# Node pass of a graph network: map pairs in one scatter, roots on ScalarE, stores issued by SyncE

## The reference, cut to what matters

```
# a layer for a node without edges (the part that the node pass computes for every node)
x1 = norm(relu(norm(x @ W1b + b1)) @ W2 + b2 + x)              # layer 0
x2 = norm(gelu(norm(x1 @ W + bias)) + x1)                      # layer 1
h  = elu(elu(elu(x2 @ Wl1 + b) @ Wl2 + b) @ Wlin + blin)       # layer 2
x3 = norm(h + x2)
x4 = norm(x3)                                                  # layer 3 adds nothing
def norm(y): return (y - mean(y)) / sqrt(var(y) + 1e-5)
```

## Time and profile before

| | us |
|---|---|
| runs | 4839.3, 4844.04, 4848.83; median 4844.04 |
| profiled execution: device time | 4839.3 |
| profiled execution: span | 4837.6 |
| node pass (from its first instructions to the first of slot pass 0) | 64.91 to 1669.33 |
| busy over the span: PE, DVE, ACT, POOL | 3813.0, 3637.8, 3183.7, 3089.0 |

### The profile page before, as it was taken

How to read it: one execution, slowest core, us unless ns; L and a number is a source line. 1 busy time by engine, 2 the same in 40 slices (tenths; PEclk the granted TensorE clock), 3 DMA queues, 4 the chain that set the end, 5 groups by cost and what they waited for, 6 DMA issues and landing times. The chain is left out here.

```text
span 4837.6 us, 74788 instructions
## 1 busy us (share of the span) xinstructions
PE 3813.0 (79%) x19896; PEld 2560.8 (53%) x20115; DVE 3637.8 (75%) x5894; ACT 3183.7 (66%) x10636; POOL 3089.0 (64%) x3645
## 2 busy tenths in 40 slices
PE   3888888888888699999688886888867777576676
PEld 3666666666666456666465564555534444344444
DVE  3666566666666488888599996999979999577776
ACT  2888888888887578888588885555545555333333
POOL 4889898898998577777444442333234443477775
PEclk9999999999999799999799998999989999788888
DMA  2334334334433333333233332333334433333221
GB/s 68 103 106 109 106 104 112 105 109 111 111 107 95 99 85 94 91 89 82 69 87 88 90 89 63 106 106 107 96 77 107 107 107 89 84 83 83 82 80 48
DMA packets 695838, 451.77 MB, mean 93 GB/s; under 512 B 143539, under 2 KB 623257, under 8 KB 695696
## 3 DMA queue, kind: packets, MB, share of 16 engines
q1 hardware_dynamic: 219504, 182.41, 14.0%
q10 hardware_dynamic: 413392, 186.30, 13.5%
q0 software_dynamic: 62800, 81.68, 7.0%
HBM read 253.00 MB, written 199.90 MB: 94 GB/s over the span
## 5 line engine op out<-in xcount | busy, mean ns | idle before, releaser
L769 POOL TENSOR_TENSOR node_rstd<-node_variance,minus_half 128x4 f32<-128x4 f32 x588 | 650.1, 1109 | 13.5 <-DMA slot_map<-node_value,node_index 1.4
L224 ACT ACTIVATE node_z<-psum 128x128 f32<-128x128 f32 x1960 | 513.5, 277 | 156.7 <-PE psum L204 87.6
L230 DVE TENSOR_TENSOR node_x<-psum,node_rstd 128x512 f32<-128x512 f32 x294 | 202.9, 690 | 487.2 <-POOL node_rstd L769 487.2
L1153 POOL DMA_INDIRECT slot_src_rows<-x,slot_index x392 | 450.8, 1150 | 168.5 <-issue 104.5
L919 POOL DMA_INDIRECT slot_map<-node_value,node_index x392 | 417.6, 1065 | 74.5 <-issue 73.5
L224 ACT ACTIVATION_READ_ACCUMULATOR node_z<-psum 128x1 f32 x1960 | 407.0, 208 | 0.0
L224 ACT ACTIVATE slot_logit<-psum 128x128 f32<-128x128 f32 x980 | 256.7, 280 | 198.0 <-PE psum L204 197.9
L1153 POOL DMA_INDIRECT slot2b_src_rows<-xl,slot2b_index x196 | 249.1, 1271 | 81.8 <-issue 46.2
L213 PE MATMUL psum<-ident,node_x 128*128 128x128 f32 x784 | 140.0, 306 | 193.9 <-DVE node_x L230 193.4
L1139 POOL DMA_INDIRECT out_nodes<-slot_new,slot_side_index x196 | 228.0, 1163 | 91.6 <-POOL slot_side_index L1133 43.8
L204 PE MATMUL psum<-center,slot_t 128*128 128x128 f32 x1176 | 215.1, 285 | 81.5 <-DVE slot_t L1592 52.7
(11 more groups left out here) (400 smaller groups left out, 12778.7 us busy)
## 6 DMA issues: line engine op xcount, KB each, us to landing
x<-node_x ACTq DMA_DIRECT2D x294, 256.0 KB, 2.7
slot_keep<-keep SPq DMA_DIRECT2D x147, 256.0 KB, 3.9
node_xT<-in_x_T SPq DMA_DIRECT2D x98, 256.0 KB, 3.4
out_nodes<-node_x ACTq DMA_DIRECT2D x98, 256.0 KB, 3.0
x<-slot_new ACTq DMA_DIRECT2D x98, 256.0 KB, 2.4
slot_dst_rows<-x SPq DMA_DIRECT2D x98, 256.0 KB, 4.3
staged<-node_gathered ACTq DMA_DIRECT2D x14, 896.0 KB, 5.9
xl<-node_xl ACTq DMA_DIRECT2D x98, 128.0 KB, 3.8
```

The lines of the kernel that those rows point to most:

```text
L224: ins = act.activation(g.z[u][:, t, :], rows[:, t, :], ACT.Square, scale=float(D ** -0.5), accum_out=g.mean_square[u][:, t:t + 1])
L230: v.tensor_tensor(out[:, :, :], source, g.rstd[u][:, :].unsqueeze(2).broadcast_to([P, TILES, D]), ALU.mult)\
L769: pool.tensor_tensor(g.rstd[u][:, :], g.variance[u][:, :], g.c.minus_half[:, :], ALU.pow).then_inc(g.pool_out[u], 1)
L1153: pool.indirect_dma_start(src_rows[u][:, t, 0:src_width], None, table, at_index(index[u][:, t:t + 1], 0))\
```

## The change

Six edits, all for the node pass:

- The two scatters per tile become one of a pair of numbers (8 bytes per node). Both orders use the index list of the last slot; the mirrored number of that target's first slot is now computed in `prepare` on DVE, and some tables there are no longer made.
- The norms `sq0`, `sq2` and `sq4` take their root on ACT (`_log`, then `_rstd` as exp). `sq1` and `sq3` stay on POOL.
- The squares of `x3` are dropped. With r the factor of the fifth norm, the variance of `x3` is 1 - eps x r^2, so DVE computes r^2 and then 1 + eps - eps x r^2 on 128x4 tiles, and POOL its power -0.5.
- All stores go to SP, in the plan's order, together with the loads. The gathered rows are stored per unit (two tiles), no longer once per iteration.
- Gathers and scatters are steps of the chain: `gather0`, `gather1`, `put0`, `put1` of every unit stand together in POOL's order.
- The order is a new plan with period 12.80. Table loads are put by the program, as in the slot passes. Wherever a table load is not needed for a step, none is put.

```
-        "node": (6.61, (2.400, 2.660, 3.600, ...), (0.01, 0.55, 1.50, 3.45, 3.86, 6.01)),
+        "node": (12.80, (4.154, 2.724, 12.612, ..., 98.077, 91.997, 97.903, 7.365, 7.370, 7.375, 7.380, 0.000), ()),

+def norm_on_act(tag, out):
+    return [("ACT", tag), ("ACT", tag + "_log"), ("ACT", tag + "_rstd"), ("DVE", out)]
+def norm_on_pool(tag, out):
     return [("ACT", tag), ("POOL", tag + "_eps"), ("POOL", tag + "_rstd"), ("DVE", out)]

+NODE_CHAIN = [("SP", "load"), ("PE", "h0")] + norm_on_act("sq0", "z0") + [("PE", "z0T"), ("ACT", "relu0"), ("PE", "y0")] + \
+    norm_on_pool("sq1", "x1") + [("SP", "store_x1"), ...] + norm_on_act("sq2", "z1") + \
...
+    norm_on_act("sq4", "x3") + [("SP", "store_x3"), ("DVE", "square"), ("DVE", "var5"), ("POOL", "rstd5"), ("DVE", "x4"),
+                                ("SP", "store_x4"), ("POOL", "gather0"), ("POOL", "gather1"), ("POOL", "put0"), ("POOL", "put1"),
+                                ("SP", "store_staged")]

# SP
+                if step == "load":
+                        sp.wait_ge(*g.PE.done(u, i - 1, "y0"))
+                    sp.dma_start(xT[u][:, :], ...).then_inc(x_loaded[u], 16)
+                elif step == "store_x1":
+                    sp.wait_ge(*g.DVE.done(u, i, "x1"))
+                    sp.dma_start(rows_in_table(dram.x1, i, u), x1[u][:, :, :]).then_inc(x1_stored[u], 16)
...
+                elif step == "store_staged":
+                    sp.wait_ge(gathers_done[u], (i + 1) * 16 * SIDE)
+                    sp.dma_start(dram.staged[...], gathered[u][:, :, :]).then_inc(staged[u], 16)

# ACT
+                elif what == "log":
+                    act.wait_ge(*g.ACT.done(u, i, tag))
+                    act_copy(act, g, u, g.variance[u][:, :], g.mean_square[u][:, :], ACT.Ln, c.eps[:, 0:1])
+                elif what == "rstd":
+                    act.wait_ge(*g.ACT.done(u, i, tag + "_log"))
+                    act_copy(act, g, u, g.rstd[u][:, :], g.variance[u][:, :], ACT.Exp, scale=-0.5)

# DVE
+                elif step == "square":
+                    v.tensor_tensor(g.raw[u][:, :], g.rstd[u][:, :], g.rstd[u][:, :], ALU.mult)
+                elif step == "var5":
+                    v.tensor_scalar(var5[u][:, :], g.raw[u][:, :], -LN_EPS, 1.0 + LN_EPS, ALU.mult, ALU.add)

# POOL
-                    pool.indirect_dma_start(dram.slot_map_flat, at_index(index[k][:, t:t + 1], 0),
-                                            value[k - 1][:, t:t + 1], None, bounds_check=2 * N - 1, ...)
+                    pool.indirect_dma_start(dram.slot_map, at_index(dst_index[:, t:t + 1], 0), value[:, t, :], None,
+                                            bounds_check=N - 1, oob_is_err=False).then_inc(scattered, 16)
+                elif step == "rstd5":
+                    pool.tensor_tensor(rstd5[u][:, :], var5[u][:, :], c.minus_half[:, :], ALU.pow)

# prepare, VectorE, at its end
+            v.tensor_scalar(c.payload[:, :, 1], first_col[:, :], -1.0, float(N_PAD + E_PAD - 1), ALU.mult, ALU.add)
```

More of the change, by code:

```diff
@@ L173, in plan @@
         steps.names = [step for of, step in chain if of == engine and not step.startswith(UNCOUNTED)]
-UNCOUNTED = ("store", "index", "gather", "dst_index", "dst_gather", "keep_map", "scatter")
+UNCOUNTED = ("store", "index", "gather", "put", "dst_index", "dst_gather", "keep_map", "scatter")
 def tiles_of(t):
@@ L627, in pe_node @@
[L627 to L674, removed]
@@ L677, in act_node @@
[L677 to L712, removed]
-    if step == "store_x3":
-        act.wait_ge(*g.DVE.done(u, i, "x3"))
-        act.dma_start(g.rows_in_table(c.dram.x3, i, u), g.x3[u][:, :, :]).then_inc(g.x3_stored[u], 16)
@@ new lines, in act_table, with table_for @@
+def act_table(act, nc, loaded, wanted):
+    if loaded not in wanted:
+        act.add_instruction(mybir.InstLoadActFuncSet(name=nc.get_next_instruction_name(), ins=[], outs=[],
+                                                     act_func_set_id=wanted[0]))
+        return wanted[0]
+    return loaded
+def table_for(step):
+    if step in ("e0", "e1"):
+        return (EXP_SET,)
+    if step.endswith("_log"):
+        return (LOG_SET,)
+    if step == "gelu1":
+        return (GELU_SET,)
+    if step.startswith("exp") or step.endswith("_rstd"):
+        return (LOG_SET, EXP_SET)
+    return None
@@ L779, in node_pass @@
         phase_tiles(ctx, nc, g, "node", NODE_STREAMS, primed=1)
-        g.A = g.B = lambda u: c.psum[:, u, :]
-        gathers = [(0, t) for t in range(SIDE_TILES)]
-        scatters = [(k, t) for t in range(SIDE_TILES) for k in (1, 2)]
-        plan(g, NODE_CHAIN, "node", gathers + scatters)
-        middle = [n for n, item in enumerate(g.order) if item[3] == scatters[4]][0]
-        g.order = [(-1, 0, "POOL", "side_index")] + g.order[:middle] + [(-1, 0, "ACT", "stage")] + g.order[middle:] + \
-            [(-1, 0, "POOL", "side_end")]
@@ L838, in run @@
+            settled = table_at_end(g)
             def run(i, part):
+                loaded = settled if part == "all" else None
                 for u, i, step in turns(g, "ACT", i, part):
-                    if step == "stage":
-                        stage(i)
-                    else:
-                        act_node(act, g, u, i, step)
-                    if step == "sq5":
-                        act.wait_ge(*g.DVE.done(u, i, "x3"))
-                        act_squares(act, g, u, g.x3[u])
@@ L862, in run @@
             def run(i, part):
                 for u, i, step in turns(g, "PE", i, part):
-                    pe_node(pe, g, u, i, step)
-            run(0, "in")
-            with pe.Fori(1, NODE_ITERS) as i:
-                run(i, "all")
-            run(NODE_ITERS, "out")
+                    work(u, i, step)
+            whole(pe, run)
         @block.vector
@@ L1280, in work @@
                         .then_inc(stored[u], 16)
-            wants = [table_for(step) for _, _, of, step in g.order if of == "ACT" and table_for(step)]
-            settled = None
-            for wanted in wants + wants:
-                settled = settled if settled in wanted else wanted[0]
+            settled = table_at_end(g)
             def run(i, part):
```

430 lines of the change are left out of this document (246 added, 184 removed), and 12 rows, old and new, of tables (NODE_CHAIN, PLAN).

## The result

| | before | after |
|---|---|---|
| median of four runs | 4843.0 us | 4551.2 us |
| profiled execution, device time | 4839.3 | 4551.07 |
| profiled execution, span | 4837.6 | 4549.4 |
| node pass in the profiled execution | 1604.4 | 1319.8 |

The ratio is 0.9399, with a 95% interval of 0.9384 to 0.9414. The changed kernel is 292 us faster; the forecast was 4593, with a range from 4543 to 4690.

What follows compares the result with a forecast made beforehand. POOL bounds the node pass now, ACT afterwards at 12.84 us per unit; 97 x 13.1 + 85 = 1356, 248 less than 1604, gives 4591 for an execution like the profiled one, 4593 as a middle, range 4543 to 4690.

Steps and rivals of the forecast that it cites:

- POOL as the bound before: Node pass of the old kernel: POOL's queue sets the pace, its groups filling 15.61 of 15.94 us per unit.
- POOL after the change: POOL's remaining powers, adds, gathers and scatters in the node pass: 8.9 us per unit, 7 less.
- the dearer scatter: Pair scatter on POOL priced at the two it replaces, 2.53 us: 11.4 us per unit, still not bounding.
- ScalarE as the next bound: ACT in the changed node pass: its work sums to a floor of 12.84 us per unit.
- Rival (c): ACT's table switches cost more than they show: ACT stays at 15.6 per unit, no change, 4833 us; chance 0.02.
- the store issues at 0.38 each: Five store issues on ACT before, 1.9 us per unit, counted in its 14.35; they leave with the change.
- PE: PE in the changed node pass: floor 11.9 us per unit at clock 1.00, 12.6 at 0.94; 1.00 expected.
- rival (a): PE or mutual waits bound the node pass: period 13.97 us, 164 us gained, 4675 us; chance 0.24.
- SP's queue: Loop through SP's in-order stores and loads: 23.3 us per two units, 11.6 each, hidden under 12.84.
- Rival (b): SP's wait ahead of the load makes the node pass slower: 17.9 us per unit, +217, 5056 us; chance 0.03.
- Period: Node pass time per unit after the change: 13.1 us, ACT's floor plus 2%.
- Ends: Fill, drain and barrier of the node pass: 85 us after the change, between 58 and 110; 58.2 before.

## Why the prediction was right, point by point

**POOL as the bound before.** Right. Taking 2.5 us per unit from POOL alone shortened the period by 2.3, and moving the stores alone shortened nothing.

**POOL after the change.** Right in size: its groups come to 9.5 us per unit with their gaps (8.9 forecast), and the pair scatter to 1.31, close to the lower bound that was taken. Wrong in one inference, that the dearer scatter at 11.4 per unit "still does not bound": with two scatters the time rose by 38 us, though POOL's sum was below ScalarE's.

**ScalarE as the next bound.** Right: 12.84 forecast, 12.71 measured, no wait for another engine, and +1.13 for 1.17 of added work. That the sum came so close was partly luck. Read from the same stretch (805.70 to 818.41), the five groups of squares take 5.37 where 5.00 was forecast; ln and exp take 1.30 (1.56), the copy of `xl` 0.26 (0.43), the two wide functions 1.46 (1.56), the three exps 1.72 (1.71) and the two table switches 2.60 (2.58). An error of +0.37 stood against errors of -0.53.

The Trainium skill, "ScalarE: Activation LUTs", section on what ACT_TABLE_LOAD costs, adds about 1.38 to each table switch. The trace again shows 1.30 for load and start of the next function together, so the estimate by the page, 2 x 1.38 = 2.8 us per unit more, would have been too high by that much. Rival (c) did not come.

**The step that failed: the store issues at 0.38 each.** "ACT had ... 14.35 before" was too high. The kernel before with one scatter has the same work on ScalarE: 12.7 us per unit busy, and 13.4 with all that is put down to "issue". In the changed kernel the five issues returned to ScalarE cost 0.28 per unit, not 1.9. The forecast's own show why: the issue of 0.38 starts at 814.88 and the table load beside it at 814.94. The claim that without the stores' move and the dropped squares "the gain would be small" is refuted too: the kernel before with one scatter has neither, and it has 230 of the 291 us. The error did not reach the forecast of the time, since the floor after the change contains no stores.

**PE.** Right that it does not bound and that the clock rises: it was 1.00 with PE busy 95%. The floor of 11.9 was 0.4 too low: PE is busy 953.0 / 77.2 = 12.3 us per unit, and 12.3 again at a period of 12.48, where it is full. So rival (a) did not come, but the margin under ScalarE's 12.7 was 0.4 and not 0.9.

**SP's queue.** No sign of the loop was seen: landings of `xT` have a median of 3.5 us and PE does not wait for them. The 2.3 us for queueing behind stores was not seen in that median. Rival (b) did not come.

**Period.** 13.1 forecast, 12.95 measured. The 2% put on the floor for waits stands for something else: no wait for another engine, but 0.24 us per unit of a gap once per iteration, which went when the loop was written out. Size: 97 x 0.15 = 15 us.

**Ends: the term that was most off.** 85 forecast, 1319.8 - 97 x 12.95 = 64 measured, within the bounds but far from the value taken. By the forecast's own test (the stage off by over 25 us; it is off by 36, of which 15 come from the period) this step was wrong. The timeline of SP shows where, in the loads of `xT` and the stores of `x4` of the first unit, of a unit in the steady part and of the last one:

```profile
70.52 0.45 SPq L706 DMA_DIRECT2D node_xT<-in_x_T  x1
144.77 0.37 SPq L721 DMA_DIRECT2D out_nodes<-node_x  x1
150.99 0.39 SPq L706 DMA_DIRECT2D node_xT<-in_x_T  x1
...
1200.04 0.38 SPq L706 DMA_DIRECT2D node_xT<-in_x_T  x1
1297.38 0.37 SPq L721 DMA_DIRECT2D out_nodes<-node_x  x1
1303.65 0.98 SPq L706 DMA_DIRECT2D node_xT<-in_x_T  x1
...
1379.81 0.37 SPq L721 DMA_DIRECT2D out_nodes<-node_x  x1
```

(The 98 loads and 98 stores are paired in order.) In the steady part a unit takes 97.3 us from load to last store, close to the 95 over which the plan spreads it. The first one takes 74.3 and the last one 76.2, where fewer units are in flight. The first nine loads also follow each other at 10.1 us and not 12.95, which saves 23. So 6.3 us before the first load, 76.2, 4.2 after the last store and -23 make the 64. The forecast took the steady length of the chain for its length at the ends, and the units at the ends run faster than that. Size: 21 us.

With 2.9 us of change in the slot passes and 0.7 in `prepare`, the period and the ends are the whole difference of 40 us between 4591 and 4551.

**Where the gain came from.** The merge of the scatters alone gives 230 of 291 us by the ratios (218 of 285 by the stages). The rest, some 60 us, needs the new order: on one chip, the same work in the old order is slower (stage 1465) than the old work with one scatter (1387). The roots on ScalarE were never tried alone, so their own share is open.

## What to carry to other kernels

When an in-order queue is the bound, price its removable work first; here halving the map scatters gave three quarters of the gain. A schedule is part of the work it was made for: moving three roots to another queue at unchanged places cost 1000 us with no engine above 62%, so after such an edit look for a ring of waits before adding up busy times. And count the gap at a loop's end on the engine that bounds.

## What the runs showed that was not expected

- DMA issues on ScalarE's queue overlap its activations: five of 0.38 us cost 0.28 us per unit in all, where their tiles were long done.
- A loop iteration of ScalarE ended in a gap of 1.7 us when nothing else held it; written out, the gaps were gone (20.3 us per 1000 to none).
- Two scatters in place of one cost 38 us although POOL had 7% to spare by its sum.
- A unit takes 97 us through the chain in the steady part, and 74 to 76 at its ends.
- One plan with roots on another queue ran at a period of 23.4 in place of 13; its cause is open beyond this: SP's wait is not its link, and six moved starts gave 2.5 us back.
